# Attention with a mixture of experts, fp32, one core: heads stacked by transfers, or parted in SBUF in stacked order and turned by PE

## What is computed

```python
x = L0_attn_x
xn = _layernorm(x, axis=-1)
x = x + _L0_attn_ref(xn, ...) + _L0_ffn_ref(xn, ...)
```

```python
kv_c = x @ W_kv                      # rank 32, then divided by its root mean square, times g_kv
q_c = x @ W_q                        # rank 64
k_content, v = heads(kv_c @ W_kdec, 8), heads(kv_c @ W_vdec, 8)
q_content = heads(q_c @ W_qdec, 8)
k_rope, q_rope = heads(x @ W_krope, 32), heads(q_c @ W_qrope, 32)   # then rotated by cos, sin
q, k = concatenate([q_content, q_rope], -1), concatenate([k_content, k_rope], -1)
scores = einsum('bhqd,bhkd->bhqk', q, k) / sqrt(40)                 # causal mask, softmax
out = einsum('bhqk,bhkd->bhqd', attn, v) @ W_o
```

## Time and profile before

| | us |
|---|---|
| median of 3 runs | 874.66 |
| lowest and highest run | 870.6, 875.03 |
| span of the profiled execution | 839.4 |
| the profiled execution's own time | not recorded beside its span |
| median less span | 35.3 |
| PE, DVE, ACT, POOL busy | 664.6, 595.0, 389.3, 289.5 |

### The profile page before, as it was taken

How to read it: one execution, slowest core, us unless ns; L and a number is a source line. 1 busy time by engine, 2 the same in 40 slices (tenths; PEclk the granted TensorE clock), 3 DMA queues, 4 the chain that set the end, 5 groups by cost and what they waited for, 6 DMA issues and landing times.

```text
span 839.4 us, 14709 instructions
## 1 busy us (share of the span) xinstructions
PE 664.6 (79%) x4646; PEld 518.4 (62%) x4646; DVE 595.0 (71%) x1632; ACT 389.3 (46%) x842; POOL 289.5 (34%) x284
## 2 busy tenths in 40 slices
PE   0456887887787877888787887878098999999996
PEld 0345665665565656666566665656066888888885
DVE  2557688676679766758767676784934776779896
ACT  0122344444443444535334453443046777777773
POOL 6452341634616343143141332325000000075674
PEclk9977899999999999999898998999688999999999
DMA  5346645456456354344334443435840577789763
GB/s 142 106 155 223 197 155 189 149 189 207 151 184 203 124 179 149 112 138 135 113 129 131 140 129 122 157 96 169 270 146 25 178 249 244 256 290 284 258 181 95
DMA packets 66051, 141.59 MB, mean 169 GB/s; under 512 B 9034, under 2 KB 34615, under 8 KB 65975
## 3 DMA queue, kind: packets, MB, share of 16 engines
q1 hardware_dynamic: 61303, 131.74, 48.5%
q0 software_dynamic: 4096, 8.40, 3.7%
q10 hardware_dynamic: 576, 0.52, 0.2%
HBM read 47.30 MB, written 29.88 MB: 92 GB/s over the span
## 4 chain that ended last, share of the span: by engine, by line
PE 45%; DVE 20%; DMA 13%; issue 7%; SPq 7%; POOL 5%; ACT 3%; POOLq 0%; ACTq 0%; DVEq 0%
DMA QK<-heads_low 10%; PE bank L1587 8%; SPq L472 6%; PE bank L1605 5%; POOL QK L694 4%; DVE heads_low L990 4%; PE bank L1359 3%; PE bank L1342 3%; PE bank L1418 2%; DVE mx L981 2%; PE bank L1609 2%; PE bank L1345 2%; PE bank L1431 2%; PE bank L1434 2%; ACT heads_high L714 2%
## 5 line engine op out<-in xcount | busy, mean ns | idle before, releaser
L981 DVE TENSOR_REDUCE mx<-bank 128x3 f32<-128x384 f32 x256 | 141.5, 553 | 81.5 <-PE bank L1434 80.7
L735 ACT ACTIVATE prob<-bank 128x384 f32<-128x384 f32 x256 | 125.8, 493 | 130.7 <-PE bank L1345 130.4
L641 POOL TENSOR_TENSOR rot<-rot,t 128x512 f32<-128x512 f32 x64 | 82.5, 1290 | 223.0 <-DVE t L973 222.9
L714 ACT ACTIVATE heads_high<-bank 120x384 fp32r<-120x384 f32 x128 | 63.0, 494 | 155.7 <-PE bank L1418 86.0
L694 POOL DMA_INDIRECT QK<-expert_outs,out_at x64 | 66.0, 1031 | 181.4 <-DMA expert_outs<-prob 162.8
L1431 PE MATMUL bank<-QK 120*128 120x256 f32 x256 | 98.7, 386 | 25.2 <-DVE heads_low L990 19.5
L990 DVE TENSOR_TENSOR heads_low<-bank,heads_high 120x384 fp32r<-120x384 f32 x128 | 70.5, 552 | 67.0 <-ACT heads_high L714 62.0
L1285 DVE TENSOR_TENSOR QK<-vaug,QK 128x512 fp32r<-128x512 f32 x124 | 86.3, 698 | 41.1 <-ACT QK L827 38.5
L1342 PE MATMUL bank<-QK 122*128 122x256 f32 x256 | 92.0, 359 | 3.0 <-DMA QK<-mT 2.8
L1418 PE MATMUL bank<-ident,rot 128*120 128x128 f32 x384 | 70.1, 296 | 28.7 <-POOL rot L641 14.2
L1434 PE MATMUL bank<-mask_qk,identb 128*128 128x256 bf16 x256 | 76.7, 300 | 0.0
(11 more groups left out here) (222 smaller groups left out, 1402.0 us busy)
## 6 DMA issues: line engine op xcount, KB each, us to landing
QK<-heads_high SPq DMA_DIRECT2D x128, 200.0 KB
wb<-weight_parts SPq DMA_DIRECT2D x46, 512.0 KB, 4.7
QK<-heads_high SPq DMA_DIRECT2D x64, 240.0 KB
QK<-heads_low SPq DMA_DIRECT2D x64, 200.0 KB
weight_parts<-wb SPq DMA_DIRECT2D x18, 512.0 KB, 5.8
QK<-heads_low SPq DMA_DIRECT2D x32, 240.0 KB
rot<-expert_rows SPq DMA_DIRECT2D x23, 256.0 KB, 4.1
expert_outs<-prob SPq DMA_DIRECT2D x23, 256.0 KB, 4.4
```

The lines of the kernel that those rows point to most:

```text
L735: act_f(prob[:, h % P_SLOTS, :], ST_PS[h % 2][:, P:4 * P], ACT.Exp, scale=SCALE).then_inc(s_exp, 1)
L981: V.tensor_reduce(mx[:, 0:3, h], B_PS[bank_of(k)][:, 0:3 * P].rearrange("p (a c) -> p a c", a=3), AX.X, ALU.max).then_inc(s_bfree[bank_of( ...
```

## The change

The attention becomes a stream of 64 groups of four heads (16 batches of 4 groups). The loop goes over beats `t` of four steps `s`; in a beat each engine works on groups of different age: group `t` is projected and rotated, `t - 1` and `t - 2` are turned, `t - 3` gets scores for the maximum, `t - 5` the transposed scores, `t - 6` its values.

- **Projection and rotation.** `project` makes, for the four heads and both tiles, queries (2 x 2 matmuls of 160 columns), keys' rotary part (2 x 3 of 128) and keys' content and values (2 x 2 of 32) into two joined banks. DVE rotates all of it in three instructions (640, 256 and 256 elements), with the cos and sin tables spread out beforehand. POOL adds.
- **Parting before turning.** ACT's `part_heads` writes the high part twice into `heads_parted` in stacked order, in one instruction with 1280 elements written; POOL's `take_low` (now on POOL, 640 elements) writes the low part between them. Each head then has its 120 stacked columns next to one another in SBUF.
- **Turning into place.** PE turns each head's 120 columns (fp32r transposes, 16 a group, 64 a batch, was 24) into a ring bank, and ACT (three units of four) and DVE (one of four) copy 512 columns of it straight into `QK`. There is no `restack`.
- **Maxima** are negated, turned and placed four heads at a time; SP issues the transfer, 64 in all instead of 32. There are 9.5 ring units per four heads, was 7.
- **Scores.** Of each pair of score matmuls the second has 128 columns instead of 256.
- **Order.** A batch's preparing steps (`turn_rows`, `small_rows`, `small_stacks`, `turn_stacks`) stand a beat apart. Loads are split by use, key and value weights go through ACT's queue, presets come later, the zero fills are issued earlier. `list_blocks` is a generator whose pieces run at beats 64 to 67, the rest after. The first half of the first hidden pass is made before the last output projection.
- Expert passes are otherwise unchanged.

```diff
+HG = 4
+PER = H // HG
+NG = B * PER
+STEPS = 4
+MAX_LAG, NEG_LAG, SC_LAG, PV_LAG = 3, 4, 5, 6
+TURN_AT = {3: (1, 0), 0: (2, 1), 1: (2, 2), 2: (2, 3)}
+FIRST, LAST = -5, NG + 7
...
+            def place_maxima(g):
+
+                k = UNIT_NO[g, ("n",)]
+                sp.wait_ge(s_bfree[bank_of(k)], freed(k))
+                at_least(sp, s_st, HG * (g - 7))
+                sp.dma_start(QK[KQ:KK, g // PER % 2, 0, heads_of(g), :].bitcast(F32), mT[:, g % 2, :].bitcast(F32))\
+                    .then_inc(s_mrow[g % 2], 16)
...
-            def restack(beta, side, i):
...
-                for row, part in enumerate((hs, hs, ls) if side == "q" else (hs, ls, hs)):
-                    sp.dma_start(QK[row * D:(row + 1) * D, beta % 2, n, heads[0]:heads[-1] + 1, :].bitcast(F32),
-                                 part[i * D:(i + 1) * D, n, 0:len(heads), :].bitcast(F32)).then_inc(s_rk[side][i], 16)
...
+            def add_turned(g):
+
+                pool.wait_ge(s_turned, g + 1)
+                rope_part = r[g % 2][:, :, :].rearrange("p o (h d) -> p (o h) d", d=D)[:, :, DC:D]
+                nc.gpsimd.tensor_tensor(rope_part, rope_part, t2[g % 2][:, :, :], ALU.add).then_inc(s_rot, 1)
+
+            def take_low(g):
+
+                pool.wait_ge(s_hi, g + 1)
+                nc.gpsimd.tensor_tensor(low_of(g), rotated(g), high_of(g), ALU.subtract).then_inc(s_lo, 1)
...
+            for t, s in beats():
+                if s == 0 and group(t - 1):
+                    take_low(t - 1)
+                if s == 2 and group(t):
+                    add_turned(t)
...
+            def put_stack(g, i):
+
+                k = UNIT_NO[g, ("t", i)]
                 sc.wait_ge(s_bfill, k + 1)
...
+                act_f(stacked(g, i), B_PS[bank_of(k)][0:KQ, :].rearrange("p (h t) -> p h t", h=HG), ACT.Copy)\
+                    .then_inc(s_bfree[bank_of(k)], 1)
...
+            def part_heads(g):
+
+                sc.wait_ge(s_rot, g + 1)
+                if g >= HL_SLOTS:
+                    sc.wait_ge(s_bfill, UNIT_NO[g - HL_SLOTS, ("t", 3)] + 1)
+                act_f(high_of(g, 2), rotated(g).unsqueeze(3).to_broadcast([P, 2, NT * HG, 2, D]), ACT.Copy).then_inc(s_hi, 1)
...
+            def rotate(g):
+
+                dve.wait_ge(s_pfill, g + 1)
+                at_least(dve, s_lo, g - 1)
+                V.tensor_tensor(r[g % 2][:, :, :], prs[:, :, 0:ROW], cos_t, ALU.mult)
+                rope_part = prs[:, :, 0:ROW].rearrange("p o (h d) -> p o h d", d=D)[:, :, :, DC:D]
+                turned = t2[g % 2][:, :, :].rearrange("p (o h) d -> p o h d", o=2 * NT)
+                hh = DR // 2
+                V.tensor_tensor(turned[:, :, :, 0:hh], rope_part[:, :, :, hh:DR], sin_t[:, :, :, 0:hh], ALU.mult)
+                V.tensor_tensor(turned[:, :, :, hh:DR], rope_part[:, :, :, 0:hh], sin_t[:, :, :, hh:DR], ALU.mult)\
+                    .then_inc(s_turned, 1)
...
+                for j in range(NT):
+                    ps = prs[:, j, 0:ROW]
+                    mm(ps, qsT[:, j, :], wqa[:, heads, :], start=True, stop=False, skip_group_check=True)
+                    mm(ps, qsT[:, j, :], wqb[:, heads, :], start=False, stop=True, skip_group_check=True)
+                for j in range(NT):
+                    ps = prs[:, NT + j, 0:ROW].rearrange("p (h d) -> p h d", d=D)
+                    xh, xl = (xhl[:, b % 2, a, j * P:(j + 1) * P] for a in range(2))
+                    mm(ps[:, :, DC:D], xh, wkr[:, 0, heads, :], start=True, stop=False, skip_group_check=True)
+                    mm(ps[:, :, DC:D], xh, wkr[:, 1, heads, :], start=False, stop=False, skip_group_check=True)
+                    mm(ps[:, :, DC:D], xl, wkr[:, 0, heads, :], start=False, stop=True, skip_group_check=True)
+                    mm(ps[:, :, 0:DC], ksT[:, j, :], wkv[:, 0, heads, :], start=True, stop=True, skip_group_check=True)
+                    ins = mm(prs[:, NT + j, ROW:ROW + HG * DC], ksT[:, j, :], wkv[:, 1, heads, :],
+                             start=True, stop=True, skip_group_check=True)
+                ins.then_inc(s_pfill, 1)
+
+            def turn_parted(g, i):
+
+                k = UNIT_NO[g, ("t", i)]
+                if i == 0:
+                    pe.wait_ge(s_lo, g + 1)
+                bank_free(k)
+                for n in range(HG):
+                    ins = nc.tensor.transpose(B_PS[bank_of(k)][0:KQ, n * P:(n + 1) * P].bitcast(F32R), parted(g, i, n),
+                                              identr[:, :])
+                ins.then_inc(s_bfill, 1)
...
+                mm(ps[:, P:3 * P], k[:, 0:P], q, start=True, stop=False, skip_group_check=True)
+                mm(ps[:, 0:P], k[:, P:T], q[:, P:T], start=False, stop=False, skip_group_check=True)
...
+            for t, s in beats():
...
+                if group(t - SC_LAG):
+                    head_scores(t - SC_LAG, s)
+                if group(t - MAX_LAG):
+                    scores_for_max(t - MAX_LAG, s)
+                if s == 0 and group(t):
+                    project(t)
+                lag, i = TURN_AT[s]
+                if group(t - lag):
+                    turn_parted(t - lag, i)
+                g = t - PV_LAG
+                if group(g) and s == (0 if g % 2 else 2):
+                    group_values(g)
+                if s == 0 and group(t - NEG_LAG):
+                    turn_maxima(t - NEG_LAG)
...
```

More of the change, by code:

```diff
@@ L37 @@
 SMALL_STEPS = 13
[L38 to L54, removed]
@@ L421, in raw_no, with pair_at, beats, ring_empty @@
-        def raw_no(beta, order, half):
-            return 8 * beta + 2 * order + half
-        def side_of(order):
-            return ORDERS[order][0]
+        def pair_at(t):
+            return (t - PV_LAG) // 2 if group(t - PV_LAG) and (t - PV_LAG) % 2 else None
+        def beats():
+            return [(t, s) for t in range(FIRST, LAST + 1) for s in range(STEPS)]
+        def ring_empty(eng):
+            for i in range(B_BANKS):
+                eng.wait_ge(s_bfree[i], (UNITS - 1 - i) // B_BANKS + 1)
@@ L601, in _ @@
         def _(pool):
[L602 to L608 removed]
+            memset = nc.gpsimd.memset
@@ L894, in normalise @@
                 at_least(dve, s_xn, b * NT)
-                for n in range(N_X):
-                    if not isinstance(b, int) or n == i // XL:
+                for n, (first, end) in enumerate(X_PARTS):
+                    if first <= i < end:
                         dve.wait_ge(s_x[n], 16)
                 for j in range(NT):
-                    at = slice(i + j, i + j + 1) if isinstance(b, int) else bass.ds(i + j, 1)
-                    steps.add(V.bn_stats(st6[:, j, :], xres[:, at, :]))
+                    steps.add(V.bn_stats(st6[:, j, :], xres[:, i + j, :]))
                 steps.need()
@@ L1082, in router @@
                     V.tensor_copy(place_of[:, ts, :], two[:, :, :]).then_inc(s_idx, 1)
+                    if q == GROUPS - 1:
+                        steps.add(V.tensor_tensor(count[:, :], found[:, q, :], ebase[:, :], ALU.add))
+                        steps.need()
+                        V.tensor_copy(fill_row[:, :], count[:, :]).then_inc(s_free, 1)
             def list_blocks():
@@ L1267, in block_low @@
+            for _ in listing:
+                pass
+            ring_empty(dve)
             def block_low(m):
@@ L1570, in turn_block, with hidden @@
                 ins.then_inc(s_xt, 1)
-            def hidden(m):
+            def hidden(m, chunks=range(FC)):
                 if m >= NP:
@@ L1583, in hidden @@
                         pe.wait_ge(s_ws, 2 * 16)
-                for c in range(FC):
+                for c in chunks:
                     at_least(pe, s_act[c], m)
```

1208 lines of the change are left out of this document (586 added, 622 removed).

## The result

The changed kernel takes 986.1 us (979.9 to 989.52, four runs) beside 873.39 for the kernel before: a ratio of 1.127, 95% interval 1.121 to 1.133. It is slower by an eighth, where 778 us were forecast.

What follows compares the result with a forecast made beforehand. No engine was full; a restack transfer each turn set the attention's pace. Start 21, first beats 25, 59 beats of 7.75 (457), last beats 37 and experts 203 made 743, plus 35.3: 778 us; 8 in 10 for 742 to 845.

Steps and rivals of the forecast that it cites:

- The step that failed: PE's holds in a beat: 0.7 us at the maximum's bank, some tenths behind DVE batch work; 0.9 us taken.
- clock 9 throughout: Sign expected in the profile after: PE's granted clock at level 9 throughout, with PE busy well above 79% in the middle.
- 1.15 was put down: PE's waits in a beat: 0.9 us for holds and 0.25 us for the router's DVE work.
- The upper bound of the beat: Beat of four heads: 7.75 us expected, at most 8.7 us if handovers cost what they cost today.
- The sum's last term: 35.3 us around the profiled span, added to the 743 us of span to give 778 us.
- 1: Rival: narrow fp32r matmuls on PE are not fast; beat 10.2 us, 923 us in all; chance 0.16.
- 2, the port: Rival: POOL or the port it shares with DVE holds the beat at 8.75 us, 837 us; chance 0.10.
- 3, the ring: Rival: the ring banks hold the beat at 8.7 us, only the ends gain, 834 us; chance 0.12.
- Rare holds: DVE's tiny steps near POOL's long operations: held only rarely, about half a us each.
- no PE stop of 20 us for listing: Before the experts: listing spread over beats 64 to 67, so PE has no idle of 20 us there.
- PE's own work: PE's issue time per beat, from scores, transposes, values, projection and the rest: 6.6 us.
- The stretch from the last projection to the experts: From the last projection to the first hidden matmul: forecast at 42 us.

Runs made afterwards that it cites:

- reads_first: Changed kernel with the step 3 batch reads put ahead of the exponential and part_heads on ACT and the maximum on DVE; 821.79 us, ratio 0.977.
- imposed_wait: reads_first with one wait added: PE's projection waits until ACT has parted the heads of the group before; 939.12 us, ratio 1.069.
- parts_last: Changed kernel with, on ACT alone, the batch reads ahead of part_heads but behind the exponential and the stack; 892.11 us, ratio 1.014.
- project_late: Changed kernel with PE's projection moved in step 0 behind the transposes and the group's values; 950.15 us, ratio 1.0815.
- both_late: reads_first and project_late together, the whole computation; 852.11 us, ratio 0.968.
- low_after_max: both_late with POOL's low part made to wait until DVE has written the negative maxima of its step; 831.26 us, ratio 0.952.

## Why the prediction was wrong

**The step that failed** is "PE is held about 0.7 us where the transpose of step 3 wants the bank of the maximum ..., and some tenths behind batch work on DVE; I take 0.9". The engines' sums were added up for each engine, and the batch steps counted in them, but the place of these steps was not followed to who waits for them. They free the banks that the next projection needs, and they stood last in step 3, behind 1.26 us of `part_heads`. The "some tenths" measured 1.35 us a beat at the projection, while the 0.7 us at the bank of the maximum were 0.01 (0.6 us in 45 beats). The second part of the same step is the clock. The prediction says "clock 9 throughout", as it took one idle stretch a turn away and saw none in its place. With 1.35 us of idle time at one spot of each beat the clock was 0.83, so 34% of the time at the lower level, and 43% of that lost: 0.34 x 0.43 x 10.66 = 1.56 us a beat; in reads_first 0.12 x 0.43 x 8.59 = 0.44. These are estimates, with the 43% of the one stretch above.

So the 2.91 us a beat over the forecast part as follows. The lower clock, put at nothing, is 1.56. PE's waits are 1.85 (1.35, and 0.50 at its other lines: 22.6 us in 45 beats) where 1.15 was put down, 0.70 more. The rest, 0.65, is PE's own issue time, some 7.25 us and not 6.6.

The difference between the two beats can be added up: wait 1.35 - 0.09 = 1.26, clock 1.12, less 0.33 that PE waits more for negative maxima in reads_first (21.1 us in 56 beats) than in the changed kernel (2.3 in 45), where it comes so late that they are mostly ready: 2.05 us, measured 2.07. The same sum for imposed_wait gives 1.09 + 0.58 - 0.37 = 1.30, measured 1.31; for parts_last and project_late it is off by 0.2 to 0.3. That the clock's fall is caused by the wait is shown by imposed_wait (0.94 to 0.88 with one wait added); how much of it each wait causes isn't: project_late waits less than imposed_wait and has the lower clock.

**The upper bound of the beat**, "8.7 if the handovers cost what they cost today", was no bound: a new order brings handovers of its own.

**The sum's last term.** 35.3 us "around the span" don't exist. On the ground of the profile, 839.4, the forecast was 743, a ratio of 0.885; the error in the ratio, 0.24, is not touched by this. ("Twelve restack DMAs a batch" is a slip too, they are 18; no term rests on it.)

**Rivals.** 1 fell: the narrow price was right within 0.02 us. 2, the port, was real but mis-sized: 1.0 us a beat was priced, the runs give 0.28 by place (both_late to low_after_max) and 0.43 with the operation cut. "Rare holds" was wrong, as was the plan to take them as a single rival at 0.10 rather than as a term. 3, the ring, has the right flavour (batch steps "now stand a beat apart"), but the waits it names are small: bank releases by `mx` cost PE 0.01 us a beat in the changed kernel and 0.06 in reads_first; only in low_after_max are they, with 0.48, the largest wait left. The cause found was none of the three.

**What held**: the first projection (21, measured 18.8), the bias turned at 12 (12.00), score pairs at 0.60 us a head, the projection's 1.56, no PE stop of 20 us for listing. PE's own work was sized too low: in low_after_max the beat of 8.23 holds 0.83 us of waits and 0.07 of lower clock, so 7.3 of issue time and not 6.6. Transposes at 0.37 to 0.45 for four instead of 0.33 are 0.15 to 0.5 of it; the rest was not itemised. The stretch from the last projection to the experts is 51 instead of 42 without the unknown waits. With the right order the kernel's beat is 0.5 us above the forecast and its gain 4.8% instead of 11%.

**Left open**: what, in the changed kernel, makes the 0.054 in ratio between it and imposed_wait. By the sum above it is 0.17 us a beat of longer wait and 0.54 of lower clock, and why the clock is lower isn't shown. The reads are there later too, and DVE's part of them behind its maximum; no run separates that from the longer wait itself.

## What to carry to other kernels

Sums of busy time per engine don't tell the pace of a software pipeline whose banks are shared by two kinds of work: list for each shared buffer who frees it, where that step stands in its engine's order, and what long operation stands ahead of it. Put small steps that free a buffer ahead of long ones that nobody waits for. Price a wait of PE that comes back at every beat with what it does to the clock (here an estimated 1.12 us of clock for 1.26 us of waiting), and keep small DVE steps clear of long GpSimd operations by order, which costs one wait.

## What was not expected of the hardware

- The clock fell after an idle stretch of PE of 1.71 us, one microsecond after PE had restarted, and stayed low for 6.5 us of full work. After the next one, of 1.99 us, up to 328.93, it didn't fall: every window of 1 us from there to 340 has 1.00. So the length of one wait doesn't tell what it costs.
- More columns on PE cost almost nothing: 0.06 us a beat for an expected 0.43 us, with the clock at 0.97 instead of 0.94.
- A DVE step of 4 elements took 1.46 us beside POOL's subtraction, and such holds weren't rare: the three steps cost 0.88 us a beat where they take 0.51 unheld.
- In some jobs ACT, DVE and POOL stop behind a queue that the profile doesn't know while POOL issues indirect DMAs, for 14.5 us at once in the changed kernel. In these jobs the kernel before takes 4% longer (875 against 841 us); that the stops are the reason isn't shown.
